# A gated cross-attention block on one core: GpSimd's share by pair, stack copies in the maxima stage, earlier loads at the end of attention

## The chip, the core and the metric

The kernel runs on one core of a Trainium2 chip. The core has TensorE (matrix products into PSUM), VectorE, ScalarE and GpSimd (elementwise work and reductions), SyncE, which here issues all the DMAs, and sixteen DMA engines. Each engine has its own instruction stream, and streams wait for each other through semaphores. The metric is the device time of one execution in microseconds (us).

## What is computed

```python
x = x + tanh(g_xattn) * xattn(layernorm(x), ctx, ctx)       # x, ctx: (8, 512, 256)
x = x + tanh(g_ffn) * ffn(layernorm(x))

def xattn(query, key, value):                               # 16 heads of 16
    q, k, v = (query @ Wq + bq), (key @ Wk + bk), (value @ Wv + bv)   # split into heads
    scores = einsum('bqhd,bkhd->hbqk', q, k) / sqrt(16)
    attn = softmax(scores.reshape(H * B, Sq, Sk), axis=0)   # over all heads AND batches
    out = einsum('hbqk,bkhd->bqhd', attn, v)
    return out @ Wo + bo

def ffn(x):                                                 # 8-bit fake quantisation
    h = act_quant(silu(act_quant(x) @ wg.T) * (act_quant(x) @ wu.T))
    return h @ weight_quant(wd).T
```

The softmax runs over the axis of heads and batches together: for each query and key, 16 x 8 = 128 exponentials are summed. So a sum needs all heads and batches of one 128x128 tile of queries and keys.

## The kernel before

**Preparation** (`prepare`) normalises `x`, makes queries, keys and values, and writes queries and keys to DRAM as `q_stack` and `k_stack`: for each chunk of 128 positions and each head, 128 rows that hold bfloat16 parts of the number, so that a product over 128 rows gives a nearly exact score. Some of those rows are copies of others. They aren't written by the preparation but copied within DRAM by `copy_rows`: per chunk three key pieces of 512 KB and two query copies of 1 MB and 512 KB.

**Maxima stage** (`maxima`). For every query and key it finds the largest score over heads and batches, from half-height tiles. It goes through eight *couples* of heads. SyncE loads the tiles of a couple one couple ahead (`load_pair`: 2 MB), TensorE multiplies, ScalarE copies three of four PSUM tiles out (L704), VectorE takes the maximum (L714, L719). Behind the tiles of couples 2 to 7 SyncE issues two of the `EARLY_COPIES`, eleven in all. Its last work is to load the first four key tiles and all sixteen query tiles of attention.

**Attention** (`attend`). There are 4 query chunks x 64 steps (4 key chunks x 16 heads); two steps, i.e. two heads, are a *pair* (128 in all), and eight pairs are a *region*, one tile of queries and keys (16 in all). For each pair
- TensorE makes four half-step scores (L894 puts in the negative maximum, L898 the products),
- ScalarE takes the exponentials into `e` (L965), a ring of 11 pairs, and also puts the negative maximum into some banks (L971),
- VectorE sums them over heads and batches (L1031), usually two pairs at a time (`GROUPS`). At the end of a region it adds the partial sums (L1038), inverts them (L1044) and copies the result to PSUM (L1046),
- GpSimd (L1013) and VectorE (L1024) multiply the pair's `e` by the reciprocal while the next region is being scored. A pair has 16 blocks of 128 elements a partition; GpSimd takes the first `POOL_BLOCKS[pair]` and VectorE the rest,
- TensorE multiplies by the values (`times_v`, L914), ten pairs behind the scores. It waits there for both scaled parts.

SyncE's stream is in order. After each scored step it loads the key tile that is four steps on (L835, 256 KB). At eighteen fixed steps (`LATE_STEPS`) it also issues half of one of the `LATE_COPIES`; near the chunk changes it loads query tiles (L849) and stores sums (L730).

**End of attention.** The last eight pairs are scaled with six blocks on GpSimd. TensorE puts the first four items of the output projection (`project_item`, L1069 and L1074) between the last `times_v`. They need the sums of chunk 0, which SyncE reads back from DRAM (`out_parts`) into the place of the query tiles (L872) after the last step's loads.

**Projection and feed-forward** (`ffn`). Sixteen items: TensorE projects, ScalarE scales by tanh (L1217), GpSimd adds `x` (L1184), VectorE takes statistics (L1253) and derives scale and shift (L1266 to L1274), ScalarE normalises (L1230). `x` is read again: chunk 0 at the end of attention into the place of the key tiles, chunks 1 to 3 in the projection's block (L1165) behind the eight stores of the last sums. Then follows the quantised feed-forward part.

## Time and profile before

| what | us |
|---|---|
| median of 3 runs (lowest, highest) | 871.96 (869.8, 874.48) |
| the profiled execution: time, span | 871.24, 869.1 |
| busy: PE, DVE, ACT, POOL | 743.2, 764.6, 683.0, 468.6 |
| maxima stage, first and last matmul (L683) | 128.3 to 306 |
| attention, first and last exponential (L965) | 312.7 to 700 |
| last matmul of `times_v` starts; projection block starts | 721.6; 724.2 |
| last output product ends | 863.7 |

The span is what lies between the first and the last instruction of the profiled execution. In rows, PE is TensorE, PEld its weight loads, DVE is VectorE, ACT is ScalarE, POOL is GpSimd, SP is SyncE. An idle time in square brackets names the instruction that ended it. Keys, queries, values, the sums that are read back and `x` of chunk 0 share one large tile, so the trace calls them all `arena`; `psX`, `psY` and `acc_last` are banks of PSUM.

### The profile page before, as it was taken

How to read it: one execution, taken by the hardware profiler on the slowest of the kernel's cores; microseconds unless marked ns; L12 is line 12 of the kernel's file. 1: busy time of each engine (PE TensorE's matmuls, PEld its weight loads, DVE VectorE, ACT ScalarE, POOL GpSimd, SP SyncE). 2: the span in 40 equal slices, each digit the busy share in tenths (PEclk: the TensorE clock that was granted, in tenths of full speed). 3: DMA queues.
4: the chain of work that ended last, by engine and by line, in shares of the span. 5: the costliest groups of instructions: out<-in, count | busy, mean ns of one | idle time of the engine just before them, and what ended most of it. 6: DMA issues, size and time to landing. Idle time of an engine off the chain costs nothing. (4 is left out here: it accounts for less than half of the span.)

```text
span 869.1 us, 20046 instructions
## 1 busy us (share of the span) xinstructions
PE 743.2 (86%) x8128; PEld 446.7 (51%) x8150; DVE 764.6 (88%) x830; ACT 683.0 (79%) x1094; POOL 468.6 (54%) x225
## 2 busy tenths in 40 slices
PE   8898787777777768899999999999999989459977
PEld 6564361122212245676676666766666668325334
DVE  4899639999999969899999999999999993758957
ACT  3454449999999977798998899988998823759973
POOL 1334453000000014889999999999999995414500
PEclk9999999999999989999999999999999999879989
DMA  9896786565655646778876787878776566100014
GB/s 298 276 321 197 239 251 130 135 167 145 146 145 122 242 130 216 255 218 270 281 227 202 253 275 249 232 205 274 241 196 200 173 213 193 50 1 1 1 49 146
DMA packets 98091, 164.30 MB, mean 189 GB/s; under 512 B 9617, under 2 KB 37009, under 8 KB 97681
## 3 DMA queue, kind: packets, MB, share of 16 engines
q1 hardware_dynamic: 98000, 163.03, 62.2%
q8 instruction: 65, 1.06, 0.5%
q14 instruction: 26, 0.20, 0.1%
HBM read 133.63 MB, written 41.94 MB: 202 GB/s over the span
## 5 line engine op out<-in xcount | busy, mean ns | idle before, releaser
L1013 POOL TENSOR_TENSOR e<-e,recip 128x1664 f32<-128x1664 f32 (+3 forms) x128 | 361.6, 2869 | 38.7 <-DVE recip L1044 38.7
L965 ACT ACTIVATE e<-psY 128x512 f32<-128x512 f32 x512 | 298.0, 647 | 40.5 <-PE psY L898 39.3
L1031 DVE TENSOR_REDUCE partial<-e 128x128 f32<-128x4096 f32 (+1 forms) x85 | 284.1, 3362 | 13.3 <-ACT e L965 13.3
L898 PE MATMUL psY<-arena 128*128 128x128 bf16 x2048 | 200.7, 221 | 0.1
L898 PEld LDWEIGHTS psY<-arena 128*128 128x128 bf16 x2048 | 149.2, 98 | 74.0 <-issue 27.8
L704 ACT ACTIVATE copies<-ps_max 128x1024 bf16<-128x1024 f32 x189 | 175.6, 1090 | 0.0
L894 PE MATMUL psY<-shift,minus 128*128 128x512 bf16 x395 | 152.6, 386 | 13.6 <-DMA arena<-k_stack 7.6
L719 DVE TENSOR_TENSOR high<-copies,high 128x3072 bf16<-128x3072 bf16 x63 | 110.3, 1750 | 0.4 <-ACT copies L704 0.4
L1004 POOL MEMSET ones_w<- 96x128 bf16 x1 | 0.2, 206 | 172.6 <-POOLq L640 172.6
L914 PE MATMUL psX<-e,arena 128*32 128x128 f32 x2048 | 76.3, 290 | 8.8 <-POOL e L1013 5.5
L1024 DVE TENSOR_TENSOR e<-e,psY 128x384 f32<-128x384 f32 (+3 forms) x128 | 80.6, 670 | 1.6
L714 DVE TENSOR_TENSOR high<-ps_max,high 128x1024 bf16<-128x1024 f32 x63 | 76.7, 1218 | 1.5 <-PE ps_max L683 1.5
L304 POOL TENSOR_TENSOR parts<-rest,parts 128x512 bf16<-128x512 f32 x32 | 37.6, 1179 | 71.4 <-ACT parts L448 71.3
L971 ACT ACTIVATE psY<-shift 128x512 f32<-128x512 bf16 x117 | 73.6, 629 | 0.0
L914 PEld LDWEIGHTS psX<-e,arena 128*32 128x32 f32 x2048 | 58.1, 110 | 18.5 <-POOL e L1013 15.9
L894 PEld LDWEIGHTS psY<-shift,minus 128*128 128x128 bf16 x395 | 38.6, 98 | 26.7 <-DMA arena<-k_stack 10.5
L683 PE MATMUL ps_max<-q_both,k_odd 128*128 128x512 bf16 x128 | 34.5, 382 | 10.9 <-DVE high L714 5.5
L683 PE MATMUL ps_max<-q_both,k_even 128*128 128x512 bf16 x128 | 34.2, 382 | 11.1 <-ACT copies L704 5.8
L683 PE MATMUL ps_max<-arena,k_odd 128*128 128x512 bf16 x128 | 34.0, 382 | 11.1 <-ACT copies L704 5.9
L683 PE MATMUL ps_max<-arena 128*128 128x512 bf16 x128 | 34.0, 382 | 10.9 <-ACT copies L704 4.8
L1443 POOL TENSOR_TENSOR arena<-up,sil 128x512 f32<-128x512 f32 x20 | 25.4, 1271 | 30.5 <-ACT up L1376 30.5
L914 PE MATMUL acc_last<-e,arena 128*32 128x128 f32 x1024 | 38.4, 291 | 1.9
(170 smaller groups left out, 1004.7 us busy)
## 6 DMA issues: line engine op xcount, KB each, us to landing
arena<-k_stack SPq DMA_DIRECT2D x256, 256.0 KB, 3.6
arena<-q_stack SPq DMA_DIRECT2D x64, 256.0 KB, 4.3
k_stack<-parts SPq DMA_DIRECT2D x40, 256.0 KB, 3.8
q_stack<-parts SPq DMA_DIRECT2D x40, 256.0 KB, 3.5
arena<-in_x_dram SPq DMA_DIRECT2D x5, 1024.0 KB, 10.1
k_stack<-k_stack SPq DMA_DIRECT2D x9, 512.0 KB, 11.2
arena<-in_ctx_dram SPq DMA_DIRECT2D x4, 1024.0 KB, 6.6
arena<-q_stack SPq DMA_DIRECT2D x8, 512.0 KB, 8.2
```

The source lines that it names most:

```text
L683: last = nc.tensor.matmul(ps[:, kc, j * S:(j + 1) * S], k_head[:, kc, b * P:(b + 1) * P], q_both[p % 2].rearrange("p c (b q) -> p c b q", ...
L704: nc.scalar.activation(dst, ps[:, kc, :], ACT.Copy).then_inc(copied, 1)
L714: nc.vector.tensor_tensor(high[:, COPIED, :], ps[:, COPIED, :], high[:, COPIED, :], ALU.max).then_inc(direct, 1)
L719: nc.vector.tensor_tensor(high[:, 0:COPIED, :], copies[:, g % RING], high[:, 0:COPIED, :], ALU.max).then_inc(updated, 1)
L894: nc.tensor.matmul(bank[:], minus[:], shift_at(qc, kc).to_broadcast([P, HB, P]), start=True, stop=False, skip_group_check=True)
L898: last = nc.tensor.matmul(bank[:, j * P:(j + 1) * P], ks[:, i % KRING, b * P:(b + 1) * P], qs[:, h, b * P:(b + 1) * P], start=False, stop= ...
L914: last = nc.tensor.matmul(acc[pair // BANK_PAIRS][grp:grp + 32, col:col + P], vpad[:, kc, b, v_col:v_col + 32], e_at(p, z, z + 1), start=F ...
L965: nc.scalar.activation(e_at(p, half * HB, (half + 1) * HB).rearrange("p q z i -> p z q i"), ps[n % SCORES][:].rearrange("p (z q i) -> p z ...
L971: nc.scalar.activation(ps[(n - 1) % SCORES][:].rearrange("p (b q) -> p b q", q=P), shift_at((p + 1) // CHUNK, (p + 1) % CHUNK // PAIRS).to ...
L1013: nc.gpsimd.tensor_tensor(part, part, by_pairs(recip[:, r % 2, :], share), ALU.mult).then_inc(pool_scaled, 1)
L1024: nc.vector.tensor_tensor(part, part, by_pairs(recip_v[:, (r % 2) * P:(r % 2 + 1) * P], BLOCKS - share), ALU.mult).then_inc(dve_scaled, 1)
L1031: nc.vector.tensor_reduce(partial[:, :, k, :], e[:, t:t + n].rearrange("p t q z i -> p q i t z"), AX.XY, ALU.add).then_inc(sum_done, 1)
```

## The change

Five edits.

1. `POOL_BLOCKS`, GpSimd's share of the eight pairs of a region, goes from (8, 14, 13, 13, 13, 13, 13, 13) to (6, 12, 12, 14, 14, 14, 15, 15). In region 0 the sums are grouped 1, 2, 2, 2, 1 pairs instead of 2, 2, 2, 1, 1.
2. All twenty row copies are issued in the maxima stage, three behind each couple's tiles from couple 1 on (two at the last). The half copies in attention and SyncE's waits for them go; instead SyncE waits for all copies before it loads the first tiles of attention.
3. ScalarE computes one exponential of a single column at the end of the maxima stage, which brings its table load with it.
4. In the last chunk, the sums of chunks 0 and 1 are read back in four halves of 512 KB, behind the key tiles of steps 52, 54, 56 and 58; those of chunk 2 come after the loop, as before, in two halves. Each waits until the sums are stored.
5. Chunks 1 to 3 of `x` are loaded before the end of attention into the first half of the value tile, once its first two key chunks have been used for the last time. GpSimd adds from there. The projection block loads only the last chunk's sums.

```diff
+STACK_COPIES = (row_copies(0, 0) + row_copies(1, 0) + row_copies(0, 1) + row_copies(0, 2) + row_copies(0, 3)
+                + row_copies(1, 1) + row_copies(1, 2) + row_copies(1, 3))
+COPIES_A_COUPLE = 3
...
-                    if p >= 2:
-                        for what in early[2 * (p - 2):2 * (p - 1)]:
+                    if p:
+                        for what in STACK_COPIES[COPIES_A_COUPLE * (p - 1):COPIES_A_COUPLE * p]:
                             copy_rows(sp, k_stack, q_stack, what, keep["k_copied"], keep["q_copied"])
-                sp.wait_ge(keep["k_copied"][0], copied_pieces(0, 0))
-                sp.wait_ge(keep["q_copied"][0], copied_pieces(1, 0))
+                for c in range(NC):
+                    sp.wait_ge(keep["k_copied"][c], 16 * len(K_COPIED))
+                    sp.wait_ge(keep["q_copied"][c], 16 * len(Q_COPIED))
                 sp.wait_ge(scored, (H - 2) * UNITS)
...
+                nc.scalar.activation(spare[:], keep["zero_w"][:, 0:1], ACT.Exp)
...
+    SUMS_STEPS = {STEPS - H + 4 + 4 * c + 2 * m: (c, m) for c in range(2) for m in range(DC)}
-    POOL_BLOCKS = (8, 14, 13, 13, 13, 13, 13, 13)
+    POOL_BLOCKS = (6, 12, 12, 14, 14, 14, 15, 15)
+    FIRST_GROUPS = ((0,), (1, 2), (3, 4), (5, 6), (7,))
...
-                        if late in LATE_STEPS:
-                            what, half = LATE_STEPS[late]
-                            copy_rows(sp, k_stack, q_stack, what, keep["k_copied"], keep["q_copied"],
-                                      slice(half * PAIRS, (half + 1) * PAIRS))
...
+                        if last and i in SUMS_STEPS:
+                            load_sums(*SUMS_STEPS[i])
...
+                def load_sums(c, m):
+                    if m == 0:
+                        sp.wait_ge(stored, 16 * B * (c + 1))
+                    sp.dma_start(keep["oT"][:, c, m], out_parts[c, m * P:(m + 1) * P].rearrange("p b q -> p (b q)")
+                                 ).then_inc(keep["o_loaded"][c], 16)
...
-                for c in range(NC - 1):
-                    sp.wait_ge(scored, 2 * (ALL - H + H // NC * (c + 1)))
-                    sp.wait_ge(stored, 16 * B * (c + 1))
-                    sp.dma_start(keep["oT"][:, c], out_parts[c].rearrange("(m p) b q -> p m (b q)", p=P)
-                                 ).then_inc(keep["o_loaded"][c], 16)
+                sp.wait_ge(scored, 2 * (ALL - H + 12))
+                for m in range(DC):
+                    load_sums(2, m)
+                sp.wait_ge(multiplied, ALL_PAIRS - 2 * PAIRS)
+                for c in range(1, NC):
+                    sp.dma_start(keep["x_rest"][:, c - 1], x_rest[c - 1]).then_inc(keep["x_loaded"][c], 16)
                 sp.wait_ge(scored, 2 * ALL)
                 sp.dma_start(keep["x_first"], x_first).then_inc(keep["x_loaded"][0], 16)
```

SyncE, start of attention. Before, the late copies stand between key tiles:

```order
L835 DMA arena<-k_stack 128x1024 x17
L72 DMA k_stack<-k_stack 8x16384
L835 DMA arena<-k_stack 128x1024 x2
...
L72 DMA q_stack<-q_stack 8x16384
L835 DMA arena<-k_stack 128x1024 x12
L849 DMA arena<-q_stack 128x1024
```

and now, where the line numbers are those of the changed kernel:

```order
L653 DMA arena<-q_stack 128x1024 x13
L633 UNCONDITIONAL_BRANCH
L818 UNCONDITIONAL_BRANCH
L853 DMA arena<-in_L_xattn_bo_dram 128x256
L828 DMA arena<-k_stack 128x1024 x49
L838 DMA arena<-q_stack 128x1024
```

The first 49 key tiles now follow each other with nothing between them.

VectorE, region 1, from the copy of the reciprocal on; a block is `x2` in the last dimension (x16 is eight blocks). Before:

```order
L1046 COPY psY<-recip 128x128
L1024 TENSOR_TENSOR e<-e,psY 128x64x16
L1024 TENSOR_TENSOR e<-e,psY 128x64x4
L1031 TENSOR_REDUCE partial<-e 128x64x2
...
L1024 TENSOR_TENSOR e<-e,psY 128x64x6 x2
L1031 TENSOR_REDUCE partial<-e 128x64x2 x2
L1038 TENSOR_REDUCE summed<-partial 128x128
L1044 RECIPROCAL recip<-summed 128x128
```

and now:

```order
L1042 COPY psY<-recip 128x128
L1020 TENSOR_TENSOR e<-e,psY 128x64x20
L1020 TENSOR_TENSOR e<-e,psY 128x64x8
L1027 TENSOR_REDUCE partial<-e 128x64x2
...
L1020 TENSOR_TENSOR e<-e,psY 128x64x2 x2
L1027 TENSOR_REDUCE partial<-e 128x64x2 x2
L1034 TENSOR_REDUCE summed<-partial 128x128
L1040 RECIPROCAL recip<-summed 128x128
```

VectorE scales more at the start of a region and less at its end.

SyncE, end of attention. Before:

```order
L835 DMA arena<-k_stack 128x1024 x27
L865 DMA wo_s<-in_L_xattn_Wo_dram 128x2x256
...
L872 DMA arena<-out_parts 128x2x1024 x3
L875 DMA arena<-in_x_dram 128x8x256
L821 UNCONDITIONAL_BRANCH
L1161 UNCONDITIONAL_BRANCH
L730 DMA out_parts<-arena 32x8x128 x8
L1165 DMA x<-in_x_dram 128x8x256
L1171 DMA arena<-out_parts 128x2x1024
L1165 DMA x<-in_x_dram 128x8x256 x2
```

and now:

```order
L828 DMA arena<-k_stack 128x1024 x20
L849 DMA arena<-out_parts 128x1024
L828 DMA arena<-k_stack 128x1024 x2
...
L849 DMA arena<-out_parts 128x1024 x2
L869 DMA arena<-in_x_dram 128x8x256 x3
L871 DMA arena<-in_x_dram 128x8x256
L817 UNCONDITIONAL_BRANCH
L1156 UNCONDITIONAL_BRANCH
L724 DMA out_parts<-arena 32x8x128 x8
L1161 DMA arena<-out_parts 128x1024 x2
```

The read-back of chunks 0 and 1 has moved between the last key tiles, and the loads of `x` have moved ahead of the block's end (the branches).

## Rows read from the trace of the kernel before

**Rows 1.** Order of time, GpSimd: start us, us, line, tiles xcount [idle before <-releaser].

```profile
486.81 23.31 POOL L1013 TENSOR_TENSOR e<-e,recip 128x1024 f32<-128x1024 f32 x8 [0.99 <-DVE recip L1044]
511.15 20.28 POOL L1013 TENSOR_TENSOR e<-e,recip 128x1024 f32<-128x1024 f32 x7 [1.03 <-DVE recip L1044]
...
706.50 12.07 POOL L1013 TENSOR_TENSOR e<-e,recip 128x768 f32<-128x768 f32 x8 [1.22 <-DVE recip L1044]
```

**Rows 2.** Order of time, VectorE, the tail of the same region.

```profile
499.49 4.42 DVE L1031 TENSOR_REDUCE partial<-e 128x128 f32<-128x4096 f32 x1 [0.23 <-ACT e L965]
503.83 1.01 DVE L1024 TENSOR_TENSOR e<-e,psY 128x384 f32<-128x384 f32 x2
504.75 4.48 DVE L1031 TENSOR_REDUCE partial<-e 128x128 f32<-128x2048 f32 x2
```

**Rows 3.** Order of time, TensorE, three `times_v` blocks.

```profile
376.10 1.18 PE L914 MATMUL psX<-e,arena 128*32 128x128 f32 x32
...
378.93 1.16 PE L914 MATMUL psY<-e,arena 128*32 128x128 f32 x32
...
495.08 1.19 PE L914 MATMUL psX<-e,arena 128*32 128x128 f32 x32
```

**Rows 4.** Order of time, VectorE, the reciprocal of regions 0, 2 and 15.

```profile
336.41 0.95 DVE L1044 RECIPROCAL recip<-summed 128x128 f32<-128x128 f32 x1
...
388.23 0.95 DVE L1044 RECIPROCAL recip<-summed 128x128 f32<-128x128 f32 x1
...
705.47 0.95 DVE L1044 RECIPROCAL recip<-summed 128x128 f32<-128x128 f32 x1
```

**Rows 5.** Stretches: busy (x) of PE PEld DVE ACT POOL; PEclk, DMA share, GB/s.

```profile
171.00:182.00 11.00, 8.75 (x32) 2.15 (x32) 11.00 (x9) 11.00 (x13) 0.00 (x0) 1.00 0.84 167
182.00:194.00 12.00, 8.80 (x35) 2.51 (x36) 12.00 (x10) 12.00 (x14) 0.00 (x0) 1.00 0.46 155
```

**Rows 6.** Order of time, end of attention and projection, three engines.

```profile
703.93 0.38 PE L1069 MATMUL psY<-bo_parts,ones_w 96*128 96x512 bf16 x1 [3.39 <-DMA arena<-out_parts]
...
722.03 1.89 PE L1074 MATMUL psY<-wo_s,arena 128*128 128x256 f32 x8
...
734.06 4.94 POOL L1184 TENSOR_TENSOR x<-xn,x 128x512 f32<-128x512 f32 x4 [3.79 <-DMA x<-in_x_dram]
...
738.57 4.04 ACT L1230 ACTIVATE xn<-x,nbias,rstd 128x256 f32<-128x256 f32 x8 [5.20 <-DVE nbias L1274]
```

**Rows 7.** Groups by line and shape, 400 to 650 us; busy us, mean ns.

```profile
L1013 POOL TENSOR_TENSOR e<-e,recip 128x1664 f32<-128x1664 f32 x63 | 190.6, 3071 | 0.0
...
L1024 DVE TENSOR_TENSOR e<-e,psY 128x384 f32<-128x384 f32 x62 | 31.6, 550 | 0.0
...
L1013 POOL TENSOR_TENSOR e<-e,recip 128x1024 f32<-128x1024 f32 x10 | 19.7, 1971 | 11.0 <-DVE recip L1044 11.0
...
L1024 DVE TENSOR_TENSOR e<-e,psY 128x256 f32<-128x256 f32 x10 | 4.1, 414 | 0.0
```

**Rows 8.** Waits, 335 to 385 us: us in total, times, longest.

```profile
PEld psY L894 <- DMA arena<-k_stack: 4.8, 6, 1.4
PE psY L894 <- DMA arena<-k_stack: 3.7, 5, 1.2
```

**Rows 9.** Line 704: ns min/median/max, first and last start us.

```profile
L704 ACT ACTIVATE copies<-ps_max x189: 1018/1032/1451, 131.6 to 306.2; 128x1024 bf16<-128x1024 f32 x189
```

**Rows 10.** Order of time, ScalarE and TensorE, first work of attention.

```profile
311.44 1.28 ACT L965 ACT_TABLE_LOAD   x1 [4.25 <-PEq L640]
...
312.01 0.63 PE L898 MATMUL psY<-arena 128*128 128x128 bf16 x4
```

**Rows 11.** Stretches at the end of attention; columns as in rows 5.

```profile
690.00:696.00 6.00, 5.83 (x105) 4.16 (x103) 5.80 (x4) 5.45 (x12) 6.00 (x3) 1.00 0.66 182
700.00:704.00 4.00, 0.61 (x21) 0.36 (x10) 4.00 (x3) 0.09 (x1) 4.00 (x2) 1.00 1.00 399
```

**Rows 12.** Page, DMA issues: count, KB each, us to landing.

```profile
k_stack<-k_stack SPq DMA_DIRECT2D x9, 512.0 KB, 11.2
```

More of the change, by code:

```diff
@@ L771, in groups @@
     def groups(r):
-        for group in GROUPS:
+        for group in GROUPS if r else FIRST_GROUPS:
             p = r * PAIRS + group[0]
@@ L941, in _ @@
                 pe.wait_ge(exped, 4 * ALL_PAIRS)
-                pe.wait_ge(keep["o_loaded"][0], 16)
+                pe.wait_ge(keep["o_loaded"][0], 16 * DC)
                 for n, p in enumerate(range(ALL_PAIRS - LAG, ALL_PAIRS)):
```

47 lines of the change are left out of this document (16 added, 31 removed).

## The prediction

> **What bounds the kernel now.** I read the page first, for the engines' shares, then the view by stretches to find the stages, and in attention (311 to 724 us of the 869.1 us span) the order of time, engine by engine. It repeats a *region*: eight pairs of heads, whose exponentials are summed on VectorE, inverted, and scaled by GpSimd (`POOL_BLOCKS` of 16 blocks) and VectorE (the rest). The reader should see three clocks that nearly agree. GpSimd: eight items in 23.31 us, then 1.03 us idle until the next reciprocal [rows 1], a period of 24.34. VectorE: one wait of 0.23 us for an exponential [rows 2], so about 24.1 us of work. And a chain through all engines: from T = 486.81 three GpSimd items, `times_v` of the third pair at 495.08 [rows 1, 3], scores and exponentials of the pair eleven further on, the reduction at 499.49 [rows 2], then VectorE without a gap until GpSimd starts again at 511.15. TensorE alone needs 2.83 us a pair where nothing holds it (376.10 to 378.93) [rows 3], 22.6 a region, so it has room. Mean period of regions 3 to 15: (705.47-388.23)/13 = 24.40 us [rows 4].
>
> Before that, the maxima stage runs on ScalarE and VectorE, busy 11.00 of 11.00 us while the DMA engines are partly idle [rows 5]. After it come the last products and the projection, where two transfers are waited for, 3.39 and 3.79 us [rows 6].
>
> **Share of GpSimd.** Its items grow from 100 to 102 blocks of 128 elements a region. From 1024 and 1664 elements, 1971 and 3071 ns [rows 7], an element costs 1.72 ns, a block 0.22 us: GpSimd's region becomes 23.31+0.44 = 23.75 us. VectorE loses two blocks: (550-414)/128 = 1.06 ns an element, 0.136 us a block [rows 7], so its work is 24.1-0.27 = 23.84. In the chain the first three items fall from 35 to 30 blocks, -1.1 us, but TensorE can't use that: it ends the last pair of a region when GpSimd does, and reaches the third pair three of its own later (3 x 2.83 = 8.5 us, against 8.27 now). That costs about 0.1, as GpSimd hardly idles any more. The tail after 499.49 holds scalings of 1+1 blocks where it held 3+3 [rows 2]: -4 x 0.136 = -0.54. Chain: 24.34+0.1-0.54 = 23.9. The three clocks now stand at 23.75, 23.84 and 23.9; as each has small waits of its own I take 23.95. **13 x (24.40-23.95) = 5.9 us saved.** Ends: 2.6 (0.2 a region, if the three hand their waits to each other) and 8.4 (0.65, GpSimd alone).
>
> Six GpSimd items of 1664 elements in a row sum with the two others to the same 23.3 us in the quiet regions, whatever VectorE does beside them, and the 768-element items take 12.07/8 = 1.51 us [rows 1], on the same line. So I price the extra blocks at their slope.
> The Trainium skill speaks against the idea: "Perfetto Trace Analysis" (§ Optimizing Scalar/DVE Operations) warns that GpSimd and VectorE share an SBUF port, so moving work between them might not help; by that the 5.9 would be lost. Its page "SBUF — State Buffer" (§ Who interferes with whom) limits this to VectorE operations with two SBUF inputs or in a 2-port mode, and the trace agrees with the narrower one.
>
> **First region.** `FIRST_GROUPS` lets VectorE reduce pair 0 alone, some 2 us earlier, but it then waits for pairs 1 and 2, whose exponentials are not there yet. The sum of the reductions stays. I take 0.2 us; ends 0 and 0.5.
>
> **Stack copies.** Eighteen half copies (6 MB) leave the key stream of attention. Ten of them stand between the key tiles of steps 16 to 36, pairs 8 to 18, which is regions 1 and 2, where TensorE waited 4.8+3.7 = 8.5 us for key tiles [rows 8]; the two periods sum to 388.23-336.41 = 51.82 us [rows 4]. Without the copies region 2 should be like the rest, 23.95, and region 1 a little longer since TensorE starts it cold, 24.4: **3.5 us saved.** The other eight stand where the mean period is 24.40 anyway and bring nothing. Ends: 1.0 (keys are late for another reason, since they flow fastest here) and 4.0.
>
> They go beside the maxima stage: 24 pieces of 512 KB instead of 12. From the 189 copies of ScalarE between 131.6 and 306.2 us, 24 a couple [rows 9], a couple lasts 22.3 us, and its tiles are asked for a couple ahead. One with 2 MB of tiles and 1.5 MB of copies used 0.84x11+0.46x12 = 14.8 us of DMA time [rows 5]; with 2 MB of copies, the most a couple gets, 14.8x4/3.5 = 16.9. So 5 us stay free. Each copy is issued behind its couple's tile loads; queued behind it are the next couple's loads, some 20 us later. SyncE's wait for all copies ahead of the first query and key tiles comes a couple before attention starts at 311.44, and those 20 loads (5 MB) need 13 us of it. Cost 0; without that cover, 1 to 3 us at the start of attention.
>
> **Early exponential table.** The load took 1.28 us, to 312.72, but TensorE's first scores ended at 312.01+0.63 = 312.64 [rows 10]. Removing it frees 0.1 us: the first exponential then waits for TensorE. In its new place it lies in the 4.25 us that ScalarE idles [rows 10].
> "ScalarE: Activation LUTs" of the Trainium skill (§ What ACT_TABLE_LOAD costs) puts a switch at about 2.66 us with its drain; by that 2.7 us would be saved. The row has 1.28, and what stands beside it decides.
>
> **Loads at the end.** Four loads of 512 KB (sums of chunks 0 and 1) now stand between the key tiles of steps 52 to 58 of the last chunk. The key stream there moves 182 GB/s at a DMA share of 0.66; a little later the same engines reach 399 GB/s [rows 11]. With the sums it is 182+173 = 355 GB/s for 12 us (512 KB every two steps, 3.03 us), under the ceiling but with little air: each sum delays the tile behind it by 1.3 us. I charge +0.5 us; ends 0 and 4 (a full 1 us a load).
>
> In return the wait of 3.39 us at 703.93 goes [rows 6]. Not all of it counts. TensorE then follows GpSimd, whose last eight items end at 706.50+12.07 = 718.57 [rows 1]; one `times_v` (1.2 [rows 3]) and the fourth projection item (2.1) follow: 721.8, where now it is 722.03+1.89 = 723.9 [rows 6]. **2.1 us saved**; late next is GpSimd. Lower end 0.5.
>
> Chunks 1 to 3 of `x`, 3 MB, are asked for before 700 us instead of after 724. With the last sums and chunk 0 they are 5 MB, at 399 GB/s 13 us: in place by about 713, ahead of the projection. So GpSimd's wait of 3.79 us at 734.06 goes. ScalarE idles 5.20 us before the normalising at 738.57, which hangs on that addition through VectorE's statistics; as 5.20 is more than 3.79, the whole passes through [rows 6]. What follows is ScalarE, GpSimd and VectorE in turn with no DMA wait. **3.8 us saved**; lower end 3.0. The last chunk's own sums are fetched with nothing beside them and have slack.
>
> **Sum.** -5.9-3.5-0.2-0.1+0.5-2.1-3.8 = -15.1. The profiled execution took 871.24 us (span 869.1), so 856.1; the median of the runs is 871.96, 0.7 higher: **856.8**. All terms at their poor ends (2.6+1.0+0.5+3.0-4) give 868.9, all at their good ends about 853.
>
> **Rivals.**
> *The balance gains nothing.* The waits only change hands and the period stays at 24.4: GpSimd has 1.03 us of slack and takes 0.44 of it, while TensorE has to catch up after the light items. For it: all three clocks lie within 0.6 us. Against: the 0.54 us leave a stretch of VectorE without a gap. Time: 856.8+5.5 = 862.3.
> *Keys arrive late at the end.* The four loads cost a full 1 us each, and regions 1 and 2 keep half of their waits: +3.5+1.7 = 862.
> *The port.* GpSimd's added blocks cost twice their slope because VectorE holds it up, as the first page warns: the region is 23.31+0.88 = 24.2, +3.3 us, 860.1. It needs GpSimd spans that vary with what VectorE does; the rows show none.
> *Slower: copies overrun the maxima stage.* A copy of 512 KB lands 11.2 us after its issue [rows 12]. If half of that, 5.6 us, were DMA time that nothing else can use, 24 pieces and eight couples of tiles at 10 us would need 24x5.6+80 = 214 us where the stage has 178: +36 us, 892. It decides from where a couple's transfers pass 22.3 us, some 3 us a piece. Against: a couple with three pieces took 14.8 us.
> *The change doesn't do what it says*: the `x` loads stand in SyncE's order behind the wait for step 252 and the last sums, so chunk 1 lands only in the projection. Half of the 3.8 would be lost: 858.7.
>
> **Chances.** Forecast 0.64, balance gains nothing 0.12, keys late 0.10, port 0.03, loads late 0.05, overrun 0.03, something unseen 0.03. The range 852.5 to 864.5 takes in all but the joint poor end and the overrun. A change under 0.5% can't be told from none here, so faster means under 867.6: 0.91; same 0.05; slower 0.04.
>
> **What would show it.** Region period 23.9 to 24.0 with GpSimd idle under 0.3 us before each region; regions 1 and 2 together near 48.3, with key waits under 2 us; no wait for a tile in the maxima stage, and attention starting at 311; the first exponential at 312.6; no wait for the sums before the first projection item, and the last `times_v` right behind GpSimd; no DMA wait in the projection. Wrong would be a period of 24.3, key waits over 2 us after 680 us, or an attention that starts after 312.

## The result, and the profile after

| | us |
|---|---|
| before: median of 4 runs (lowest, highest) | 871.44 (869.8, 874.48) |
| after: median of 4 runs (lowest, highest) | 858.05 (856.41, 859.72) |
| after divided by before, with its 95% interval | 0.9842 (0.9809 to 0.9876) |
| the profiled execution of after: time, span | 859.72, 857.6 |

By the ratio the change makes the kernel 13.8 us faster (1.58% of 871.44, interval 1.24 to 1.91%). The forecast was 856.8 us, and 1.25 us separates it from the median. Total times of one kernel scatter by 3 to 11 us from run to run, however, so a total says little about the terms of a sum. So I cut the span at instructions that every kernel has. This is the table by which everything below is judged:

| stretch, us | before | after | difference | forecast |
|---|---|---|---|---|
| first exponential starts at | 312.73 | 312.12 | -0.61 | -0.1 |
| first exponential to reciprocal 0 | 23.68 | 23.24 | -0.44 | -0.2 |
| reciprocals 0 to 2 (regions 1 and 2) | 51.82 | 48.48 | -3.34 | -3.5 |
| reciprocals 2 to 14, mean of 12 | 24.396 | 24.080 | -3.79 in all | -5.4 |
| reciprocals 14 to 15 (last region) | 24.49 | 25.78 | +1.29 | -0.45+0.5 |
| reciprocal 15 to projection block | 18.76 | 16.74 | -2.02 | -2.1 |
| block to its first normalising | 14.34 | 10.50 | -3.84 | -3.8 |
| normalising to the maximum of `x` | 28.59 | 28.60 | 0 | 0 |
| maximum of `x` to the end | 101.94 | 103.18 | +1.24 | 0 |

From the first exponential to the maximum this is 454.43 us before and 442.30 after: 12.1 us where 15 were forecast.

How well a stretch repeats can be read from the kernels of the experiments whose edits don't touch it. Near the end it repeats closely: 16.72 to 16.77 us from the last reciprocal to the projection block wherever TensorE isn't held up there, 10.50 to 10.52 to the first normalising where `x` is there in time, 28.58 to 28.62 to the maximum. Elsewhere it doesn't: with the new share and the copies in the maxima stage, regions 1 and 2 take 47.83 to 48.70 us, the mean region is 24.005 to 24.143 (1.7 us over twelve), the first region takes 23.1 to 24.4 and the part after the maximum 100.0 to 103.2, though no edit reaches those. Each kernel has one profile, so a difference below these ranges isn't shown by one pair.

Order of time, kernel after, GpSimd: start us, us, line, tiles xcount [idle before <-releaser]. The rows answer [rows 1].

```profile
457.88 47.47 POOL L1009 TENSOR_TENSOR e<-e,recip 128x768 f32<-128x768 f32 x16 [0.60 <-DVE recip L1040]
505.89 16.82 POOL L1009 TENSOR_TENSOR e<-e,recip 128x768 f32<-128x768 f32 x6 [0.54 <-DVE recip L1040]
...
650.09 47.46 POOL L1009 TENSOR_TENSOR e<-e,recip 128x768 f32<-128x768 f32 x16 [0.34 <-DVE recip L1040]
699.61 12.10 POOL L1009 TENSOR_TENSOR e<-e,recip 128x768 f32<-128x768 f32 x8 [2.07 <-DVE recip L1040]
```

Sixteen items, two regions, are run together because no visible wait lies between them: 47.47/2 = 23.74 us a region at 102 blocks (23.75 forecast). The shape shown is that of the first item. The idle time at a region's start, 1.09 us on average over the twelve regions before, is now between 0 and 1.01, 0.34 on average; 23.74+0.34 is the mean region of 24.08. At the very end it is 2.07: GpSimd waits for the last region's reciprocal.

The same view, VectorE (the reciprocals of regions 0, 2, 14 and 15 and one reduction), answers [rows 4]:

```profile
335.36 0.95 DVE L1040 RECIPROCAL recip<-summed 128x128 f32<-128x128 f32 x1
...
383.84 0.95 DVE L1040 RECIPROCAL recip<-summed 128x128 f32<-128x128 f32 x1
...
672.80 0.95 DVE L1040 RECIPROCAL recip<-summed 128x128 f32<-128x128 f32 x1
...
688.35 4.42 DVE L1027 TENSOR_REDUCE partial<-e 128x128 f32<-128x4096 f32 x1 [1.78 <-ACT e L961]
...
698.58 0.95 DVE L1040 RECIPROCAL recip<-summed 128x128 f32<-128x128 f32 x1
```

Waits of the kernel after, 680 to 700 us: us in total, times, longest. The third row is the 1.78 us just seen. The first two rows are the same three stops seen twice, on TensorE's weight load and on its first matmul behind it, so they must not be added.

```profile
PEld psY L890 <- DMA arena<-k_stack: 2.8, 3, 1.1
...
PE psY L890 <- DMA arena<-k_stack: 2.3, 3, 0.9
...
DVE partial L1027 <- ACT e L961: 1.8, 1, 1.8
```

Order of time again, TensorE and then GpSimd and ScalarE at the end of attention and in the projection; they answer [rows 6]:

```profile
695.07 0.38 PE L1065 MATMUL psY<-bo_parts,ones_w 96*128 96x512 bf16 x1 [0.27 <-DMA gates<-in_L_ffn_clip_down_dram]
...
711.76 1.20 PE L910 MATMUL acc_last<-e,arena 128*32 128x128 f32 x32 [0.30 <-POOL e L1009]
...
713.12 1.89 PE L1070 MATMUL psY<-wo_s,arena 128*128 128x256 f32 x8
```

```profile
716.40 7.40 POOL L1176 TENSOR_TENSOR x<-xn,arena 128x512 f32<-128x512 f32 x6 [0.44 <-ACT xn L1208]
...
725.82 4.04 ACT L1221 ACTIVATE xn<-x,nbias,rstd 128x256 f32<-128x256 f32 x8 [1.37 <-DVE nbias L1265]
```

The waits of 3.39 us for the sums and of 3.79 us for `x` are gone, and ScalarE idles 1.37 us before normalising instead of 5.20. The last `times_v` now waits for GpSimd and for nothing else.

ScalarE at the start of attention, against [rows 10], and its copies of the maxima stage, against [rows 9]:

```profile
299.09 7.54 ACT L697 ACTIVATE copies<-ps_max 128x1024 bf16<-128x1024 f32 x8
306.64 1.28 ACT L698 ACT_TABLE_LOAD   x1
307.94 0.20 ACT L698 ACTIVATE spare_exp<-zero_w 128x1 f32<-128x1 bf16 x1
312.12 0.61 ACT L961 ACTIVATE e<-psY 128x512 f32<-128x512 f32 x1 [3.98 <-PE psY L894]
```

```profile
L697 ACT ACTIVATE copies<-ps_max x189: 1018/1032/1453, 131.1 to 305.6; 128x1024 bf16<-128x1024 f32 x189
```

The copies span 174.5 us, as before, with twice as many row copies beside them. From 153.3 us on a couple of 22.3 us uses 13.6 to 15.6 us of DMA time (a share of 0.61 to 0.70), where 16.9 were reckoned; the first one uses 18.1 (0.81).

### The profile page after: what moved, and what is told of

Same layout as the page of the kernel before. It is cut to its first block and busy times, and to the rows that moved or that the text cites. A ratio compares the mean times of both kernels' runs of the same rounds, so it can differ in the third digit from the quotient of the medians.

```text
span 857.6 us, 20062 instructions
## 1 busy us (share of the span) xinstructions
PE 745.7 (87%) x8150; PEld 448.8 (52%) x8150; DVE 757.3 (88%) x830; ACT 680.7 (79%) x1095; POOL 475.2 (55%) x225
## 5 line engine op out<-in xcount | busy, mean ns | idle before, releaser
L1009 POOL TENSOR_TENSOR e<-e,recip 128x1792 f32<-128x1792 f32 (+3 forms) x128 | 368.1, 2913 | 25.8 <-DVE recip L1040 25.7
L1027 DVE TENSOR_REDUCE partial<-e 128x128 f32<-128x2048 f32 (+1 forms) x85 | 284.2, 3360 | 11.8 <-ACT e L961 11.6
L1020 DVE TENSOR_TENSOR e<-e,psY 128x256 f32<-128x256 f32 (+3 forms) x128 | 76.4, 637 | 1.6
```

The lines of the kernel that those rows point to most:

```text
L1009: nc.gpsimd.tensor_tensor(part, part, by_pairs(recip[:, r % 2, :], share), ALU.mult).then_inc(pool_scaled, 1)
L1020: nc.vector.tensor_tensor(part, part, by_pairs(recip_v[:, (r % 2) * P:(r % 2 + 1) * P], BLOCKS - share), ALU.mult).then_inc(dve_scaled, 1)
L1027: nc.vector.tensor_reduce(partial[:, :, k, :], e[:, t:t + n].rearrange("p t q z i -> p q i t z"), AX.XY, ALU.add).then_inc(sum_done, 1)
```

## Experiments

Two questions drove them. Is the gain of each part the one it was forecast to be, or do the totals agree by luck? And where did 3 us of the expected gain go? Theory A is the forecast's: three clocks of a region near 23.9 us, copies that cost regions 1 and 2 their keys, loads that cost little. The rivals were that the share gains nothing, and that what is lost at the end comes from the four loads between the last key tiles. In the tables of results, "stretch" refers to the cut above.

### The old share in the new kernel

```diff
-    POOL_BLOCKS = (6, 12, 12, 14, 14, 14, 15, 15)
+    POOL_BLOCKS = (8, 14, 13, 13, 13, 13, 13, 13)
```

> The changed kernel with the old shares of GpSimd (8, 14, 13, ...), all else as changed. In the changed kernel regions 2 to 14 last 24.08 us each (383.84 to 672.80, twelve intervals). Theory (three clocks: GpSimd 23.3 + idle, VectorE 24.1, chain 24.34): they go back to 24.3 to 24.4, GpSimd idles 1.0 us a region again, and the kernel is 3 to 4 us slower than the changed one. Rival (the waits only change hands, the gain came from the copies that left): the regions stay at 24.1 and the time within 1 us.

Measured: 864.12 us (10 runs; ratio to before 0.9939, interval 0.9909 to 0.9969). The mean of the 12 regions is 24.383 us, that of the kernel before, and GpSimd shows its old rhythm:

```profile
459.52 23.33 POOL L1009 TENSOR_TENSOR e<-e,recip 128x1024 f32<-128x1024 f32 x8 [1.06 <-DVE recip L1040]
483.84 23.30 POOL L1009 TENSOR_TENSOR e<-e,recip 128x1024 f32<-128x1024 f32 x8 [0.98 <-DVE recip L1040]
```

From first exponential to maximum it takes 446.35 us, 4.05 more than the kernel after. The share does gain; "the balance gains nothing" falls. Regions 1 and 2 take 49.88 us without a single wait for keys. So of the 3.34 us gained there, by this pair 1.9 come with the copies and 1.4 with the share. And under the old share the early read-back does what was forecast: the end takes 16.74 us instead of 18.76, and the last region, with all four loads between its keys, 24.51 us, no more than before (24.49).

### The share alone, in the kernel before

```diff
-    POOL_BLOCKS = (8, 14, 13, 13, 13, 13, 13, 13)
+    POOL_BLOCKS = (6, 12, 12, 14, 14, 14, 15, 15)
```

> The kernel before with the new shares of GpSimd and nothing else. Theory (clocks of 23.75, 23.84 and 23.9 us, and waits for key tiles that now count since TensorE has no slack): regions 3 to 15 last 24.0 to 24.15 on average instead of 24.40, more in those that hold copies or query loads; GpSimd idles 0.2 to 0.6 us a region; the kernel is 3 to 5 us faster than before. Rival (waits change hands): 24.3 to 24.4 and no difference that can be measured.

Measured: 866.07 us (10 runs), ratio 0.9958 (0.9934 to 0.9981), mean region 24.108 us, regions 1 and 2 49.71. That confirms the share from the other side. But one stretch surprised me: the end, from reciprocal 15 to the block, is 16.72 us, as short as in the kernel after, though sums are read back here as late as in the kernel before. TensorE, share alone, in order of time:

```profile
699.07 0.38 PE L1069 MATMUL psY<-bo_parts,ones_w 96*128 96x512 bf16 x1 [2.39 <-DMA arena<-out_parts]
699.28 1.89 PE L1074 MATMUL psY<-wo_s,arena 128*128 128x256 f32 x8
...
714.63 1.19 PE L914 MATMUL acc_last<-e,arena 128*32 128x128 f32 x32 [0.17 <-POOL e L1013]
```

and the kernel before, whose first item stands in [rows 6]:

```profile
704.14 3.05 PE L1074 MATMUL psY<-wo_s,arena 128*128 128x256 f32 x8
707.12 1.62 PE L914 MATMUL acc_last<-e,arena 128*32 128x128 f32 x32
...
719.70 2.18 PE L914 MATMUL acc_last<-e,arena 128*32 128x128 f32 x64
```

Both wait for the sums, 2.39 and 3.39 us. With the shorter wait TensorE catches up and is again waiting for GpSimd at 714.63. With the longer one the same eight matmuls take 3.05 instead of 1.89 us, and the granted clock says why (stretches of the kernel before; busy of PE PEld DVE ACT POOL, PEclk, DMA share, GB/s):

```profile
698.00:702.00 4.00, 2.43 (x47) 1.64 (x44) 4.00 (x4) 2.09 (x4) 4.00 (x2) 1.00 0.94 318
702.00:704.00 2.00, 0.07 (x1) 0.10 (x2) 2.00 (x2) 0.00 (x0) 2.00 (x2) 1.00 1.03 408
704.00:706.00 2.00, 2.00 (x7) 1.65 (x7) 1.93 (x3) 0.00 (x0) 1.28 (x1) 0.68 1.02 418
706.00:708.00 2.00, 2.00 (x23) 1.17 (x26) 1.93 (x3) 0.00 (x0) 1.50 (x2) 0.50 1.05 377
```

After its 3.39 us of idling TensorE was granted half its clock (0.50, that is 1.2 of 2.4 GHz) for some 3.4 us. The item and the group behind it lost 1.16+0.43 = 1.6 us by it. So the 2.0 us of this stretch are not the price of the late read-back as such: with a wait 1.0 us shorter and no half clock, the new share alone has none of them. Why the clock fell after the one wait and not after the other isn't shown; the next kernel but one has a half clock behind a stop of 1.92 us.

### The row copies back in attention

```diff
-                        for what in STACK_COPIES[COPIES_A_COUPLE * (p - 1):COPIES_A_COUPLE * p]:
+                        for what in EARLY_COPIES[2 * (p - 2):2 * (p - 1)]:
...
+                        if late in LATE_STEPS:
+                            what, half = LATE_STEPS[late]
+                            copy_rows(sp, k_stack, q_stack, what, keep["k_copied"], keep["q_copied"],
+                                      slice(half * PAIRS, (half + 1) * PAIRS))
```

> The changed kernel with the eighteen half copies back in the key stream of attention (and eleven copies in the maxima stage, two a couple), all else as changed. Theory (the copies delay the key tiles behind them): regions 1 and 2 last 51 to 52 us together instead of 48.48, with 7 to 9 us of key waits between 335 and 385 us, and the kernel is 3.3 us slower; the maxima stage is unchanged. New point: since the new shares leave TensorE no slack, the eight copies of the later steps, which cost nothing before, cost 0.3 to 1 us in regions 4, 5 and 8, 9. Rival (keys are late because they flow at full pace there): 48 to 49 us and no difference.

Measured: 859.45 us, ratio 0.9879 (0.9825 to 0.9933). Key waits in regions 1 and 2 are back (6.7 us by the two rows together, 3.7 of it on the weight loads, against none), and yet they take only 49.03 us where the kernel after takes 48.48 and the forecast was 51 to 52. So under the new share the copies cost about 0.6 us here (1.2 by the share-alone kernel, 49.71), little more than the scatter of this stretch (47.83 to 48.70 without copies); under the old share it was 1.9. The forecast cost in the later regions that hold copies doesn't show either: regions 4, 5, 8 and 9 take 23.91, 24.35, 24.00 and 23.92 us, against 23.91, 24.32, 24.16 and 23.93 in the kernel after. The total can't tell this kernel from the one after.

### The sums read back behind the keys

```diff
-                        if last and i in SUMS_STEPS:
-                            load_sums(*SUMS_STEPS[i])
...
+                for c in range(2):
+                    for m in range(DC):
+                        load_sums(c, m)
                 sp.wait_ge(scored, 2 * (ALL - H + 12))
```

> The changed kernel with the sums of chunks 0 and 1 fetched after the last key tile instead of between the key tiles of steps 52 to 58; x still early. Theory (the four loads cost the last region 1.7 us, and their absence costs the first projection item a wait of about 3 us, of which 2 count): last region 24.1 to 24.5 instead of 25.78, wait before the first projection item 2 to 4 us, projection block 1.5 to 2 us later after the last reciprocal: total within 0.7 us of the changed kernel. Rival (the last region is long for another reason, e.g. its ring and its split reductions): last region stays above 25.5 and the kernel is 2 us slower.

Measured: 858.07 us (854.41 to 859.51), ratio 0.9865 (0.9815 to 0.9914), no slower than the change. The last region takes 24.01 us instead of 25.78, with no wait for keys in it. The end takes 20.51 instead of 16.74, and at first I put that down to the late sums. TensorE's rows speak against it:

```profile
694.99 0.38 PE L1066 MATMUL psY<-bo_parts,ones_w 96*128 96x512 bf16 x1 [2.26 <-DMA arena<-out_parts]
...
710.74 0.92 PE L911 MATMUL acc_last<-e,arena 128*32 128x128 f32 x24 [0.31 <-POOL e L1010]
713.57 0.45 PE L911 MATMUL acc_last<-e,arena 128*32 128x128 f32 x8 [1.92 <-issue]
713.96 0.52 PE L1066 MATMUL psY<-bo_parts,ones_w 96*128 96x512 bf16 x1
714.27 3.49 PE L1071 MATMUL psY<-wo_s,arena 128*128 128x256 f32 x8
```

The wait of 2.26 us for the sums has been made good by 710.74, where TensorE waits for GpSimd like everyone else. The time is lost later: 1.92 us in the middle of a group, before the last 8 of its 32 matmuls, waiting for nothing that the profile shows ("issue"), and 1.60 us because the item behind runs at half clock (3.49 instead of 1.89). Together 3.5 of the 3.8 us. The same gap at the same matmul is 0.42 us in the kernel of quarter loads and 1.03 us in the last but one kernel below, and missing in the other eleven profiles. In the three that have it, the bulk loads of `x` had ended 0.4 to 1.7 us before the gap, and the later they ended, the longer it is (here the DMA share is 1.10 until 710 us, 0.68 from 710 to 712 and 0.05 behind); in the kernel after they end near 708, over 4 us before the same matmul. But in the kernel with two later sums they end some 2 us before it, hardly earlier than in the kernel of quarter loads, and there is no gap. That the engine's own instructions came late behind these loads would fit, but nothing here shows it.

### Half of the sums, in quarters

```diff
-                            load_sums(*SUMS_STEPS[i])
+                            load_quarter(*SUMS_STEPS[i])
...
+                for m in range(DC):
+                    load_sums(1, m)
...
```

> The changed kernel with only the sums of chunk 0 between the key tiles of steps 52 to 58, as four loads of 256 KB, and those of chunk 1 after the last key tile. Theory (a key tile waits for the bytes ahead of it, so half the bytes cost under half the wait): last region 24.3 to 24.8 instead of 25.78, no wait before the first projection item, total 1.0 to 1.5 us faster than the changed kernel. Rival (the wait hangs on the number of loads or on the stream itself): last region 25.5 or more, same total.

The four loads at these steps are now quarters of 256 KB, all of chunk 0's sums; those of chunk 1 follow the last key tile. Measured: 857.96 us (ratio 0.9867, 0.9814 to 0.9921); last region 24.87 us, end 17.36 (with the gap of 0.42 us). VectorE waits 0.86 us for an exponential instead of 1.78, and the last region lies just above the forecast of 24.3 to 24.8. That looks like half the bytes and half the delay, but it isn't shown: two kernels with all the bytes at these steps, the one with `x` in the projection block and the one with the old groups (both below), have waits of 0.91 and 0.93 us and last regions of 24.91 and 24.93.

### The loads of `x` back in the projection block

```diff
-                for c in range(1, NC):
-                    sp.dma_start(keep["x_rest"][:, c - 1], x_rest[c - 1]).then_inc(keep["x_loaded"][c], 16)
...
+                    sp.dma_start(keep["x_rest"][:, 0], x_v[1]).then_inc(x_loaded[1], 16)
...
+                    for c in (2, 3):
+                        sp.dma_start(keep["x_rest"][:, c - 1], x_v[c]).then_inc(x_loaded[c], 16)
```

> The changed kernel with chunks 1 to 3 of x loaded in the projection block again, as before, behind the stores of the last sums. Theory: GpSimd waits 3.5 to 4 us for chunk 1, and all of it arrives at the first normalising, which starts 14.3 us after the block instead of 10.5; 3.8 us slower than the changed kernel. Rival (the projection is bound by TensorE's items or by the last chunk's sums and takes up the wait): under 1 us slower.

Measured: 863.52 us (9 runs), ratio 0.9913 (0.9878 to 0.9947). GpSimd and ScalarE in the projection:

```profile
725.45 4.95 POOL L1177 TENSOR_TENSOR x<-xn,arena 128x512 f32<-128x512 f32 x4 [4.32 <-DMA arena<-in_x_dram]
...
729.96 4.04 ACT L1222 ACTIVATE xn<-x,nbias,rstd 128x256 f32<-128x256 f32 x8 [5.73 <-DVE nbias L1266]
```

The wait for `x` is back (4.32 us), and the idle time before normalising with it. The stretch to the first normalising is 14.86 us against 10.50. All of the wait passes through, as forecast, and everything after it stays as long as it was. The median is 5.5 us above that of the change; 4.4 of it is this stretch. (The late loads give 14.34 us in the kernel before and 14.80 in the share-alone kernel, so their price is 3.8 to 4.4 us.)

### No early exponential

```diff
-                nc.scalar.activation(spare[:], keep["zero_w"][:, 0:1], ACT.Exp)
```

> The changed kernel without the single exponential at the end of the maxima stage, so that the table load of 1.28 us stands ahead of attention's first exponential again. Theory (TensorE's first scores end 0.1 us before the load does): first exponential 0.1 us later, total the same. Rival (a switch costs 2.66 us with its drain): 1.3 to 2.7 us slower.

Measured: 857.33 us, ratio 0.9849 (0.9806 to 0.9891); from first exponential to maximum 443.12 us, and the first exponential starts at 311.91, no later than in the kernel after (312.12). But the start of attention scatters from 311.5 to 315.3 us over the kernels, because the maxima stage starts anywhere from 127.1 to 130.2. Counted from the start of ScalarE's last copy in that stage, the first exponential comes 6.51 to 6.52 us later in every kernel with the early one and 6.58 us later in the three without: the change is worth 0.06 us where 0.1 was forecast. The table load of 1.28 us lies in idle time in either place. The Trainium skill, "ScalarE: Activation LUTs" (§ What ACT_TABLE_LOAD costs), adds a drain to it and comes to about 2.66 us for a switch. The row has its 1.28, and the switch directly behind the copies, where ScalarE was busy, shows no drain: the copies end at 306.63 us and the next exponential starts at 307.94, 1.31 us later. There the measurement differs from the page and decides.

### More still for GpSimd: 108 blocks

```diff
-    POOL_BLOCKS = (6, 12, 12, 14, 14, 14, 15, 15)
+    POOL_BLOCKS = (8, 13, 13, 14, 15, 15, 15, 15)
```

> The changed kernel with shares (8, 13, 13, 14, 15, 15, 15, 15), 108 blocks a region, so that GpSimd alone sets the pace and the price of a block can be read. Theory (0.21 to 0.22 us a block, whatever VectorE does beside it): eight items in 25.0 to 25.1 us, regions of 25.1, no idle time on GpSimd. Rival (VectorE holds GpSimd up at a shared port): more than 0.3 us a block, items of over 25.7 us that vary from region to region.

Measured: 868.32 us (one run); mean region 24.991 us. GpSimd no longer stops, here for 26 items:

```profile
518.70 81.74 POOL L1009 TENSOR_TENSOR e<-e,recip 128x1792 f32<-128x1792 f32 x26
```

That is 3.14 us an item, 25.1 for eight of these, and 25.02 to 25.17 us for the eight items of each region. The slope of 0.22 us a block gives 23.31+8x0.22 = 25.07 for 108 blocks. So the price is straight from 100 to 108 blocks, and the rival of a shared port falls for these operations. "Perfetto Trace Analysis" of the Trainium skill (§ Optimizing Scalar/DVE Operations) warns that work moved between these two engines might gain nothing; for these operations the trace does not bear that out. Two blocks moved gained time, eight lost it, since GpSimd alone then sets the period.

### No query loads in attention

```diff
-                            load_q(qc + 1, Q_STEPS[i])
+                            pass
...
-                            load_q(qc, Q_STEPS[i + STEPS])
+                            pass
...
-                            pe.wait_ge(q_loaded[h], (qc + 1) * 16)
+                            pe.wait_ge(q_loaded[h], 16)
```

> The changed kernel without the query loads of chunks 1 to 3 (48 loads of 256 KB): the queries of chunk 0 are used four times, so this part of the computation is left out. It asks where the mean region of 24.08 comes from, since the clocks gave 23.75, 23.84 and 23.9. Theory (key tiles behind query tiles are late, and the new shares leave TensorE no slack to make it up): key waits in the twelve regions after the second go from 5.6 us to under 1 us and the mean region to 23.85 or less, with only the two patterns 23.7 and 23.9 to 24.0 left. Rival (the balance itself costs 24.08: bank clearing, split reductions, catching up): mean stays above 24.0.

Measured: 857.27 us (one run). Over the 12 middle regions the waits for keys fall from 5.6 to 0.2 us (weight loads and matmuls together, so that many stops count twice; one row is left), and the mean from 24.080 to 23.992 us, where 23.85 or less was forecast:

```profile
PEld psY L894 <- DMA arena<-k_stack: 0.2, 1, 0.2
```

and in the kernel after, 384 to 674 us:

```profile
PEld psY L890 <- DMA arena<-k_stack: 3.0, 7, 0.6
...
PE psY L890 <- DMA arena<-k_stack: 1.7, 5, 0.5
...
PEld psY L894 <- DMA arena<-k_stack: 0.9, 3, 0.4
```

So 12x0.088 = 1.1 us of the middle's missing 1.6 go with these waits. One pair alone wouldn't show it, as the kernel with two later sums, whose middle regions have all their query loads, has 24.005. But its waits happen to be short too, and over all nine profiles with the new share and no copies in attention the mean region follows the waits:

| key waits in the 12 regions, us (both rows) | 0.2 | 2.1 | 3.8 | 4.3 | 5.6 | 6.4 | 6.5 | 6.7 | 8.1 |
|---|---|---|---|---|---|---|---|---|---|
| mean region, us | 23.992 | 24.005 | 24.038 | 24.059 | 24.080 | 24.116 | 24.125 | 24.130 | 24.143 |

With the old share it doesn't: 5.6 us of waits and 24.396 in the kernel before, 1.8 and 24.383 in the kernel of the first experiment. With nearly no waits the mean is still above the 23.95 of the forecast; those 0.04 us a region (0.5 us in all) have another cause, which no run here names. The two kernels with the new share and row copies in attention have 9.7 us of waits and 24.105 and 24.108 us, less than the table would suggest, so not every wait counts alike. The last region, with the four sums in its stream, stays long (25.41).

### Two sums later, two behind the keys

```diff
-    SUMS_STEPS = {STEPS - H + 4 + 4 * c + 2 * m: (c, m) for c in range(2) for m in range(DC)}
+    SUMS_STEPS = {STEPS - KRING - 3: (0, 0), STEPS - KRING - 1: (0, 1)}
...
+                for m in range(DC):
+                    load_sums(1, m)
```

> The changed kernel with the sums of chunk 0 alone in the key stream, as two loads of 512 KB behind the key tiles of steps 57 and 59, and those of chunk 1 after the last key tile. What the runs so far show: with the four loads the last region lasts 25.78 us where key tiles are late 9.4 us into it (VectorE waits 1.78 us ahead of the reduction of pairs 4 and 5), but 24.02 where a tile is late 18.7 us into it. Theory (only a tile that pair 5 or an earlier one needs lengthens the region): last region 24.0 to 24.1, any key wait lies after 15 us, first projection item without a wait over 0.5 us, 16.8 us from the last reciprocal to the projection; 1.5 us less than the changed kernel in the stretch from the second to last reciprocal to the projection. Rival (the sums then come too late for the first item): 18.5 to 20 us from the last reciprocal to the projection, no gain.

Measured: 858.49 us (6 runs, 854.98 to 863.72), ratio 0.9859 (0.982 to 0.9898). VectorE, last region:

```profile
684.55 4.42 DVE L1029 TENSOR_REDUCE partial<-e 128x128 f32<-128x4096 f32 x1
...
694.78 0.95 DVE L1042 RECIPROCAL recip<-summed 128x128 f32<-128x128 f32 x1
```

The reduction that waited 1.78 us has no wait. Last region 23.99, end 16.76: 40.75 us where the kernel after has 42.52. From first exponential to maximum it takes 438.84 us, the shortest of all kernels, 3.5 less than the kernel after; 1.8 of it lies in the two stretches that the edit touches, the rest in regions before it, within their scatter. The medians can't show it, as runs scatter by more than that.

### The same, with TensorE kept busy before the feed-forward part

```diff
                     pe.wait_ge(s["y_scaled"], NT // 2)
+                    spin(nc, 52, psY[:, 0, :], wT[:, 0, 0, 0:P], wT[:, 0, 0, 0:BANK])
                     pe.wait_ge(s["xmax_ready"], 1)
```

> As c2_later_sums, and TensorE computes 52 products that nobody reads behind the last projection item and the first transposes, where it sat idle for 15 us until the maximum over all of x was known. In that wait the granted clock falls to half in every profile, and in that of the changed kernel it fell once more about 12 us into the feed-forward part, whose length was 103.18 us against 101.94 before. Theory (the fall comes from TensorE's idleness): the clock stays at full speed through the wait and the start of the feed-forward part, which then takes 100 us or less; 1 to 3 us faster than c2_later_sums. Rival (the start is bound by the other engines and the clock costs nothing, or the products run past the maximum): no difference, or up to 2 us slower.

Measured: 859.45 us (6 runs, 854.91 to 862.09), ratio 0.9864 (0.9825 to 0.9902). What comes after the maximum takes 99.90 us; the kernel it is built on took 102.67, but kernels without the 52 matmuls range from 100.0 to 103.2. The clock stays at full speed through the wait, as forecast, but falls once the feed-forward part has begun (below), and the time doesn't change measurably. It has the gap of 1.03 us (end 17.97).

### The first region in the old groups

```diff
-        for group in GROUPS if r else FIRST_GROUPS:
+        for group in GROUPS:
```

> The changed kernel with region 0 summed in groups of 2, 2, 2, 1, 1 pairs as before. Theory (VectorE starts 2 us earlier with the new groups and gives nearly all of it back in one wait): from the first exponential to the first reciprocal 23.4 to 23.6 us instead of 23.24, nothing else changes. Rival (the earlier start counts): 25 us.

Measured: 863.01 us (one run, its own before 870.07). First exponential to reciprocal 0: 23.89 us, 0.3 above the forecast. The two other kernels with the old groups have 23.68 (before) and 24.22 (share alone). With the new groups it is 23.24 in the kernel after and 23.11 to 24.39 in the ten others, median 23.4. The middles differ by 0.5 us, in the forecast's direction, but the ranges overlap: a small gain is likely and not shown.

## Why the prediction held, and where it did not

**Share of GpSimd (-5.9).** The mechanism is right: old share 24.383, new share 24.080, and the same pair on the kernel before (24.396 and 24.108). GpSimd's own clock came out to the digit, 23.74 against 23.75. The step that was mis-sized is "I take 23.95": the measured period is 0.13 longer, 1.6 us over 12 regions, of which 1.1 go with waits for keys. In the kernel before, TensorE had room to absorb such waits (5.6 and 1.8 us of them gave the same period); with the three clocks together, more waits mean a longer region, in all nine kernels of the table above. The forecast named this room and did not ask what had been using it. GpSimd idles 0.34 us a region on average and not under 0.3; without the key waits it is 0.25.

**Regions 1 and 2 (-3.5).** The sum is right (48.48 against 48.35), its split is not. The term was given to the copies, but its target of 24.4+23.95 already contained the new period. Measured, 0.6 to 1.9 us belong to the copies and 1.4 to 2.1 to the share, by which of the two is taken away first; the stretch scatters by 0.9 us where nothing in it is changed. The forecast also misread its waits: 4.8+3.7 us [rows 8] are one row for the weight loads and one for the matmuls right behind them, which stop for the same tile (at 337.13 us, for instance, both end a wait), so TensorE stood for some 4.8 us and not for 8.5. At most 1.9 us of that counted. The term itself did not use the 8.5.

**First region, early table (-0.3).** -0.44 in the profiles for the region, of which the groups may have given 0.2 to 0.5. The table's load is hidden in both places, and moving it gave 0.06 us. The 0.61 us by which attention starts earlier in the table above is scatter of what comes before.

**Copies beside the maxima stage (0).** Right: its copies span 174.5 us, no wait for tiles, attention starts on time. The overrun is excluded.

**Loads between the last keys (+0.5).** Too small. The new share without them makes the last region 24.01 and 23.99 us long; with all four at these steps it is 25.78 here, and 24.02, 24.91, 25.78, 25.41 and 24.93 in the others. That is 1.8 us in the profiled pair and 1.1 on average, within the range of 0 to 4 but at least twice what I took. The delay of a tile was too small, too: the key tiles behind the four sums land 4.79, 6.21, 6.50 and 5.28 us after their issue, those ahead of the first sum after 2.7 to 3.1, so they took 2 to 3.7 us longer and not 1.3. Part of that is covered by asking four steps ahead. What is left stops TensorE at 682.14, 685.94 and 689.77 us (0.74, 1.01 and 1.07 us on its weight load). The first two add up to 1.75, and the reduction at 688.35 waits 1.78; the third comes behind it and costs nothing. It is so in the other kernels: stops of 0.78 to 0.88 us some 9 us into the region go with waits of 0.86 to 0.93, one of 1.48 with 1.40, one of 1.69 with 1.78. With the copies back, a stop of 0.65 us gave no wait, and 1.8 us of waiting 18.7 us into the region left it at 24.02. That key waits of over 2 us after 680 us would be a sign of error, the prediction had said itself, and its rival of late keys came true in part. Under the old share the same four loads cost nothing (24.51), so this too is slack that the new share took away.

**End of attention (-2.1).** The size is right (-2.02), the reason incomplete. It assumed that the wait for the sums itself makes TensorE late. Share alone and sums behind the keys have waits of 2.39 and 2.26 us that TensorE makes good. In the kernel before, 3.39 us was too long, and half clock added 1.6. Under the old share the early read-back is worth its 2.0 us and costs nothing; beside the new share it bought nothing that the share did not already give in the two profiles without it (the 20.51 us with the sums behind the keys hold the gap of 1.92 us and the half clock behind it), at the price of 1.1 to 1.8 us. The two terms were forecast as if they simply added up.

**Loads of `x` (-3.8).** Right to 0.1 us in the profiled pair, and the mechanism is shown by putting them back, which costs 4.4.

**The rest.** The kernel's feed-forward part differed by +1.24 us in the two profiled executions, and the median of the runs lies 1.7 us under the profiled one. That the median came within 1.25 us of 856.8 is therefore partly luck: between the first exponential and the maximum of `x` the sum was 3 us too good, and its two causes are named above.

## What to carry to other kernels

When several engines' clocks in a loop are brought together, price the slack that disappears: list the small waits that one of them had been hiding (here key tiles behind other transfers) and charge them to the new period. For a transfer slipped between others, ask which consumer sees the accumulated delay and how long before its deadline; with two of the four loads 6 us later and two behind the last tile, the same bytes were free. And judge the parts of a change by stretches between fixed instructions, not by totals, but find out first how well each stretch repeats: here from 0.05 us (end of attention) over 1 to 2 us (regions 1 and 2, the twelve regions together) to 3 (after the maximum), where totals scatter by 3 to 11.

## What the hardware showed that I had not expected

After a wait of 3.39 us TensorE ran at half clock, after ones of 2.39 and 2.26 us it did not. The length of the last stop alone doesn't decide it, though: behind the gap of 1.92 us in the kernel with the sums behind the keys the clock is halved as well (PEclk is the third column from the end).

```profile
712.00:714.00 2.00, 0.43 (x9) 0.21 (x10) 0.00 (x0) 0.00 (x0) 0.00 (x0) 1.00 0.05 17
714.00:716.00 2.00, 2.00 (x10) 1.56 (x7) 0.00 (x0) 0.60 (x1) 0.00 (x0) 0.52 0.00 0
```

The same at a longer wait, ahead of the feed-forward part (kernel after):

```profile
742.00:746.00 4.00, 0.00 (x0) 0.00 (x0) 3.30 (x15) 1.62 (x4) 2.79 (x3) 0.80 0.00 0
746.00:750.00 4.00, 0.00 (x0) 0.00 (x0) 3.71 (x19) 3.75 (x9) 0.00 (x0) 0.50 0.00 0
...
758.00:762.00 4.00, 4.00 (x23) 2.28 (x23) 0.95 (x2) 2.02 (x4) 0.00 (x0) 0.99 0.00 0
762.00:766.00 4.00, 2.28 (x12) 0.93 (x10) 1.51 (x2) 4.00 (x7) 2.12 (x2) 1.00 0.00 0
766.00:770.00 4.00, 2.49 (x13) 1.06 (x14) 2.58 (x4) 0.20 (x2) 0.37 (x1) 0.79 0.00 0
770.00:774.00 4.00, 4.00 (x19) 2.16 (x18) 1.58 (x3) 3.30 (x6) 1.27 (x1) 0.79 0.01 2
```

The clock is back at 758 us and falls a second time between 766 and 774, behind a stretch of 4 us with 2.28 us of matmuls. The kernel with two later sums has no such second fall (1.00 from its 758 on), though it has a stretch with only 2.05 us, and its part after the maximum is 0.5 us shorter. That the second fall costs this time isn't shown: the old share in the new kernel has the fall and 102.04 us. The kernel with 52 spare matmuls keeps 1.00 through the wait and then falls, after a stop of 1.70 us and in the next one, of 1.03:

```profile
750.00:754.00 4.00, 4.00 (x20) 1.82 (x19) 3.79 (x10) 3.98 (x9) 0.00 (x0) 1.00 0.00 0
...
758.00:762.00 4.00, 2.97 (x9) 0.76 (x8) 1.14 (x5) 1.26 (x2) 0.19 (x1) 0.59 0.01 2
```

Second, a gap of 0.4 to 1.9 us in the middle of a group of matmuls, always before the last 8 of the same 32, with nothing that the profile shows as its cause, in three kernels of fourteen. It stays open.
